# Message-passing layers on one core: the cast of counted pairs with its source block as the outermost loop

## The reference

```python
h = gelu(x @ W_pre + b_pre)
aggr = segment_sum(h[src] * edge_attr, dst)           # layer 0
x1 = x + aggr
y = gelu(gelu(x1 @ W1 + b1) @ W2 + b2)
x2 = layernorm(x + x1 + y)
deg = segment_sum(1, dst); dinv = rsqrt(max(deg, 1))  # layer 1
t = x2 @ W_lin.T + b_lin
agg = segment_sum(t[src] * dinv[src] * dinv[dst], dst)
out = layernorm(x2 + relu(agg + x2 @ W_root.T + b_root))
```

## Time and profile before

| | |
|---|---|
| time of the runs, median of 3 | 1157.41 us (1156.54 to 1158.27) |
| time of the profiled execution | 1149.79 us |
| its span | 1147.9 us |
| PE, DVE, ACT, POOL busy | 936.0, 740.9, 499.1, 839.1 us |
| 600 whole casts of pairs, line 963 | 757 ns each, first start 106.3 us, last 751.7 us |
| 791 gathers, line 873 | 989 ns each, first start 60.4 us, last 1082.3 us |

### The profile page before, as it was taken

The page is one execution under the profiler, slowest core; times in us unless marked ns, Lnnn a source line. Parts: engine busy times, 40 slices in busy tenths (PEclk is TensorE's granted clock), DMA queues, the critical chain, the costliest instruction groups (busy, mean ns, idle before and its releaser), DMA issues. The chain is left out here.

```text
span 1147.9 us, 20834 instructions
## 1 busy us (share of the span) xinstructions
PE 936.0 (82%) x7455; PEld 826.2 (72%) x8122; DVE 740.9 (65%) x1462; ACT 499.1 (43%) x845; POOL 839.1 (73%) x908
## 2 busy tenths in 40 slices
PE   6745766577666877987999999999999999598796
PEld 6744544455444855865888898899999999497786
DVE  8277877578677687686766767724346465445656
ACT  2304866557665675675666666520000010101116
POOL 7787777777777777777777777777777777777503
PEclk9867988778888998998999999999999999798998
DMA  8632876567566778877998999899889889476724
GB/s 225 167 104 68 299 257 214 186 202 252 185 205 192 245 241 282 264 250 251 293 296 274 294 288 316 261 300 277 255 245 282 262 235 257 109 199 176 189 71 100
DMA packets 185718, 260.24 MB, mean 227 GB/s; under 512 B 68650, under 2 KB 163882, under 8 KB 179018
## 3 DMA queue, kind: packets, MB, share of 16 engines
q1 hardware_dynamic: 158328, 215.57, 58.2%
q0 software_dynamic: 26992, 42.82, 15.4%
q10 hardware_dynamic: 290, 0.45, 0.1%
HBM read 173.12 MB, written 85.62 MB: 225 GB/s over the span
## 5 line engine op out<-in xcount | busy, mean ns | idle before, releaser
L873 POOL DMA_INDIRECT gath<-table_h,srcs x791 | 782.7, 989 | 241.1 <-issue 235.9
L1549 PE MATMUL bank_q<-piece_raw,early_late 128*96 128x250 bf16 x3453 | 405.7, 271 | 7.6 <-DVE early_late L1142 5.0
L1549 PEld LDWEIGHTS bank_q<-piece_raw,early_late 128*96 128x96 bf16 x3453 | 372.2, 123 | 2.0 <-issue 0.6
L963 ACT CAST counts_raw<-bank_q 128x490 bf16<-128x490 f32 x400 | 281.2, 757 | 145.0 <-PE bank_q L1527 142.7
L1527 PE MATMUL bank_q<-hots_raw 128*128 128x245 bf16 x834 | 162.4, 290 | 46.2 <-ACT counts_raw L963 37.3
L1286 DVE TENSOR_TENSOR msg<-gath,edg 128x480 f32<-128x480 f32 x166 | 108.1, 651 | 130.4 <-DMA gath<-table_h,srcs 116.3
L963 ACT CAST counts_raw<-bank_b 128x490 bf16<-128x490 f32 x200 | 151.4, 757 | 77.1 <-PE bank_b L1527 73.0
L1383 DVE TENSOR_TENSOR hots_raw<-counters,kb 128x1960 bf16<-128x1960 bf16 (+1 forms) x157 | 182.2, 1161 | 0.0
L1495 PE MATMUL seg<-onehot,msg 128*97 128x128 f32 (+1 forms) x830 | 120.5, 299 | 44.2 <-DVE msg L1286 42.2
L1495 PE MATMUL seg_odd<-onehot,msg 128*97 128x128 f32 (+1 forms) x832 | 118.4, 295 | 34.1 <-DVE msg L1286 31.5
L1527 PEld LDWEIGHTS bank_q<-hots_raw 128*128 128x128 bf16 x834 | 68.5, 102 | 87.5 <-ACT counts_raw L963 74.3
(11 more groups left out here) (213 smaller groups left out, 650.2 us busy)
## 6 DMA issues: line engine op xcount, KB each, us to landing
counts_hbm<-counts_raw SPq DMA_DIRECT2D x50, 1531.2 KB
piece_raw<-counts_hbm SPq DMA_DIRECT2D x250, 250.0 KB, 4.3
edg<-in_edge SPq DMA_DIRECT2D x166, 240.0 KB
gath<-table_h,srcs POOLq DMA_INDIRECT x791
piece_raw<-counts_hbm SPq DMA_DIRECT2D x38, 125.0 KB, 3.9
piece_raw<-counts_hbm SPq DMA_DIRECT2D x25, 187.5 KB, 3.2
counts_raw<-counts_hbm SPq DMA_DIRECT2D x4, 625.0 KB, 6.8
table_h<-stage SPq DMA_DIRECT2D x12, 192.0 KB, 3.1
```

Source lines behind the costliest of these rows:

```text
L873: pool.indirect_dma_start(gath[0:k, u % GS * UT + j, :], None, table[0], bass.IndirectOffsetOnAxis(ap=srcs[0:k, t:t + 1], axis=0)).then_in ...
L963: act.copy(counts[:, k % 2, :, i * WD:(i + 2) * WD].rearrange("p a (w n) -> p w a n", w=2), counted).then_inc(s_kept, 1)
L1549: mm = pe.matmul(sums(r)[0:D, 0:DN], parts[:, FINE[c] + i, part, :], rows, start=(first and i == 0 and part == 0), stop=(last and i == til ...
```

## The change

`keep_pair` views both sides of the cast in another order of loops. Before: window w, source block a, node n on both sides. After: source block a, window w, node n. The counts written are the same, to the same places. For the whole cast the two windows of five counts stand next to each other in `counts_raw`, so that with the windows inside the source block they make one run of ten.

```diff
             def keep_pair(m):
-                counted = pair_bank(m)[:, 0:2 * KC].rearrange("p (w a n) -> p w a n", w=2, n=WD)
+                counted = pair_bank(m)[:, 0:2 * KC].rearrange("p (w a n) -> p a w n", w=2, n=WD)
...
                 if k_last == k:
-                    act.copy(counts[:, k % 2, :, i * WD:(i + 2) * WD].rearrange("p a (w n) -> p w a n", w=2), counted
+                    act.copy(counts[:, k % 2, :, i * WD:(i + 2) * WD].rearrange("p a (w n) -> p a w n", w=2), counted
                              ).then_inc(s_kept, 1)
                 else:
-                    act.copy(counts[:, k % 2, :, i * WD:], counted[:, 0])
-                    act.copy(counts[:, k_last % 2, :, 0:WD], counted[:, 1]).then_inc(s_kept, 1)
+                    act.copy(counts[:, k % 2, :, i * WD:], counted[:, :, 0])
+                    act.copy(counts[:, k_last % 2, :, 0:WD], counted[:, :, 1]).then_inc(s_kept, 1)
```

## The result

The changed kernel took 1160.8 us (median of 20 runs, 1153.97 to 1168.55), the kernel before 1157.47 us (20 runs, 1151.16 to 1160.26). The ratio is 1.0032, with a 95% interval of 1.0016 to 1.0048: slower by 3.3 us, where I had forecast no change. The spread is a result too. Single executions of the same kernel lie 9 to 15 us apart, and the three runs known beforehand (1156.54 to 1158.27 us) had not shown that. The profiled execution after took 1159.72 us (span 1157.9 us).

The account below looks back on a forecast made before the run. POOL's gathers, one every 1.25 us, to about 1067 us plus a fixed 81 us tail bound the kernel. Change on the path 0: 1149.8 us, plus 7.6 us to the median, less 0.4 us, gives 1157.0 us; range 1153.5 to 1160.5 us.

Parts of the forecast that it names:

- POOL paces the kernel, slack of 25 us, path of 0 for the cast: Line 873's gathers start every 1.25 us, unheld; consumers have four units (25 us) of slack; cheaper casts change the path by 0.
- I carry that difference over: The runs' median, 1157.4 us, lay 7.6 us above the profiled execution's 1149.8 us; this was added to the forecast unchanged.
- the runs' own spread (1156.5 to 1158.3 us): Scatter of the runs known beforehand, taken as one of the inputs to the forecast range.
- 0.2% for what a measurement can tell: A measurement of this kernel was said to tell about 0.2% (2.3 us) from no change.
- a mean of line 873 that moved by 0.003 us or more: Sign of being wrong: slower or faster indirect gathers, 791 x 0.003 = 2.4 us.
- Plus a fixed tail: After DVE's last wait for a gather, about 1067 us, 81 us of last products, dense sums and finals stay constant.
- a tail that is not 81 us: Sign of being wrong: another length from DVE's last gather wait to the end, for example at another granted clock.
- The cast, 0.70 us in 0.66 to 0.85: Line 963's cast, 0.757 us before, was to take 0.70 us, between 0.66 and 0.85 us.
- about 2 ns a break: Price of each break between written runs in ACT's casts: 0.19 us over 97 breaks, 0.11 us over 48.
- `kb` row: Profile row of a 512-element cast to every second bfloat16, 0.739 us; if the type costs that, the change gains only 0.02 us.
- Together 11 us at most: PE's 186 waits for casts, 54 us, might each shrink by 0.06 us.
- 0.4 us off: Subtracted for a rival: less consumer lag disturbs line 873's gathers less, 1148.4 us at full strength; chance 0.10.

Follow-up runs that it names:

- b1_before: The kernel before, unchanged, run again beside the kernel before on the same chip: 1156.71 us, ratio 1.0004.
- b2_before: The kernel before, unchanged, run once more as a kernel of the study: 1155.81 us, ratio 0.9990 to the kernel before beside it.
- c1_one_run: Against the changed kernel, the cast writes its 490 counts in one run, window by window (output wrong): 1156.62 us, ratio 1.0000 to the kernel before.
- c2_runs_of_one: Against the kernel before, casts and half casts write single counts, source block innermost, 250 bytes apart: 1857.35 us, ratio 1.6092.

## Why the prediction was wrong

By the comparison that counts it was wrong: 1160.8 us lies above my upper end of 1160.5 us, and the interval of the ratio does not hold 1. Point by point:

- **POOL paces the kernel, slack of 25 us, path of 0 for the cast:** this held. ACT was busy 56 us less, POOL was never held, PE waited less. DVE's waits for gathers, which I had expected above 116 us, were 107.5 to 132.2 us in the six traces. One run, 49, or 98 of them: the time is the same within the interval. A cast of 2.6 us does reach the end.
- **The step that put the time outside** is the last one: "I carry that difference over", and a range from "the runs' own spread (1156.5 to 1158.3 us)", with 0.2% for what a measurement can tell. This leaves out that a whole group of executions can lie higher than another group of the same kernel. The first 20 executions of the changed kernel did, by 3.8 us against 60 later ones, and of this 2.4 us go with a gather pace of 1.252 us in place of 1.249. I had listed the sign of this ("a mean of line 873 that moved by 0.003 us or more"; it moved from 989 to 993 ns), and gave it no place in the range. Single executions scatter more than I took, too: the kernel before alone went from 1147.84 to 1165.99 us later, with a standard deviation of 2.7 us.
- **"Plus a fixed tail":** wrong. I counted 81 us from DVE's last wait for a gather (1067.2 us) to the end. This wait ends at 1053.7 and 1055.1 us in `b1_before` and `b2_before`, with 99 and 103 us behind it, and at 1064.2 us with 94 us behind it in the first trace after. I had listed "a tail that is not 81 us" as a sign of being wrong, without a price. So the stretch behind that wait is not of fixed length, nor is it paced by gathers alone, and part of it depends on the clock: 45.6 us from the turn to the end in my trace, 49.9 to 51.9 us in all other traces of the two kernels. I noted that the profile was 7.6 us below the median and carried this over as a constant, though it was the sign that this execution's end was not the usual one. That the median was met later (the means are 1156.6 us before and 1157.2 us after, forecast 1157.0) was luck in this: the usual long tail was inside the 7.6 us that I added without knowing what they were. For the same reason the tail is not what put the 1160.8 us outside.
- **The cast, 0.70 us in 0.66 to 0.85:** wrong. It took 0.638 us. The step that failed is "about 2 ns a break", taken the same for 97 and 48 breaks, and the weight given to the `kb` row. By the medians, one run is 576 ns, 49 runs 623 ns (47 ns over 48 breaks, 1.0 ns each), 98 runs 740 ns (164 ns over 97 breaks, 1.7 ns each), 490 runs of one 2621 ns (4.2 ns each). These runs lie 250 bytes apart, and their price depends on their length. It depends on the distance too, or on something that goes with it: in `kb`, whose single elements are 4 bytes apart, a break costs 0.3 ns. bfloat16 as a type costs nothing: 490 counts in one run took 0.576 us, and the line through the float32 copies gives 0.57. The sentence of the Trainium skill ("ScalarE: Activation LUTs", Step-by-step) that float32 and bfloat16 cost alike, measured there for activation functions, agrees with this row. What I took for a price of the type in the `kb` row is then left for its stepped writes; no run varied them.
- **"Together 11 us at most" for PE's waits:** wrong, they shrank by 31 us (54 to 22.7). I let each of 186 waits shrink by 0.06 us, but the cast gained twice that and 117 of the waits went away whole. Nothing of it reached the end.
- **"0.4 us off", the less disturbed gathers:** not seen. In the first trace after, line 873 took 0.973 us in 200 to 500 us, 1.000 us in 600 to 900 us and 0.971 us in 900 to 1083 us, where before had 0.964, 0.989 and 0.987. In all six traces of the changed kernel they are 0.964 to 0.984, 0.986 to 1.000 and 0.962 to 0.989, in the three of before 0.964 to 0.974, 0.989 to 0.990 and 0.980 to 0.991: no clear difference that goes with the cast. The disturbance itself is there: in the trace of before 54 of the 72 gathers that took more than 1.1 us overlap a `msg` product in time, and only 139 of the 719 others do.
- **What stays open:** shown is that the 3.3 us of the first comparison are not a property of the changed cast that returns (five repeats), and that 2.4 us of the trace's difference are a gather pace of 3 ns more, which no other trace of either kernel had. Why the gathers had this pace then, and where the rest came from, is not known: the record does not tell on which chip that comparison ran, and has no second trace from it. A cost of 0.1% and less stays open as well.

The version that beats both is the kernel with PE kept busy: 0.9944 to 0.9952 of the time before, with either cast.

## What to carry to other kernels

Ask first who sets the pace, and count the slack in units up to the place where an edit bites; here an engine with a third of its time idle, working for one that had 25 us of slack, was spared 0.12 us an instruction 600 times without any effect. Before a range is written, ask for the scatter of single executions and of whole groups of them, repeat a comparison of 0.3% before explaining it, and when the one profile at hand is far off the median, look in it for what is not usual. Short waits of PE just before a stretch that is bound by PE can be worth more than their own length: 38 small idle matmuls, in waits of 1.4, 1.4 and 1.7 us, took 6 us off.

## What the runs showed of the hardware

- A cast of ScalarE from PSUM to SBUF, 490 float32 to bfloat16 in one run: 0.576 us; in 49 runs of ten, 0.62 us; in 98 runs of five, 0.74 us; one by one, 2.6 us (medians; the runs 250 bytes apart). Whether it reads PSUM in a row or in 98 pieces makes no difference that can be seen (615 and 614 ns).
- The same casts one behind another start 0.46, 0.50, 0.58 and 2.12 us apart (medians of `c1_one_run`, after, before, `c2_runs_of_one`), less than they last.
- The cast of `kb`, every second bfloat16 written, took 0.739 us, 0.15 us over the copy of as many float32.
- TensorE's level (2.4 or 1.2 GHz) behind a wait of 1.7 us differs between executions of one kernel. The first 60 matmuls of line 1630 took 3.46 us in two of eleven traces and 4.97 to 6.38 us in the others, in which 1.2 GHz was granted for 10 to 14 us beginning 0.6 to 1.7 us behind the start of the turn. They took 3.46 us in all four traces of usual length in which PE ran idle matmuls at the turn.
- The start-to-start time of indirect gathers was 1.249 us (median) in all traces but one, which had 1.252 us.
